# Rotary embedding of the query tiles moved behind the head's softmax bound in a fused attention and feed-forward kernel

## The chip, the cores and the metric

The kernel runs on the 8 cores of one Trainium2 chip. Each core computes one batch element, with no exchange between cores. The metric is the device time of the slowest core, in microseconds (us).

## What is computed

The layer normalises x once and adds attention and a feed-forward block side by side:

```python
xn = _layernorm(x, axis=-1)
x = x + _L0_attn_ref(xn, W_q, W_k, W_v, W_o) + _L0_ffn_ref(xn, w_gate, w_up, w_down, s_gate, s_up, s_down)
# attention: 16 query heads, 4 key/value heads, head size 128, 2048 positions
Qr = _apply_rope(Q, positions)      # r0 = x0*cos - x1*sin ; r1 = x0*sin + x1*cos
Kr = _apply_rope(K_rep, positions)
scores = jnp.einsum('bhqd,bhkd->bhqk', Qr, Kr) / HEAD_DIM ** 0.5
weights = jax.nn.softmax(scores, axis=-1)
out = jnp.einsum('bhqk,bhkd->bhqd', weights, V_rep) @ W_o   # heads joined first
# feed-forward: int8 weights with one scale per output column
gate = silu(_qmatmul(x, w_gate, s_gate)); up = _qmatmul(x, w_up, s_up)
_qmatmul(gate * up, w_down, s_down)
```

## The kernel before, in words

All activations lie transposed, with features on the 128 partitions. The program has three stages. Stage 0 (until about 230 us) loads x, computes the layer norm and transposes it into `xn`. Stage A is K and V projection (until about 376 us) and then attention, head by head. Stage B (from about 1920 us) is the feed-forward block and the output projection over four tiles of 512 positions.

The change lies in the loop over the 16 heads `h` of stage A. One head is built like this:

- **Q projection.** For each tile `t` of 512 positions (NT = 4), 16 matmuls (L421) fill PSUM bank `ps_sc[:, t]`. `norm_max` (L285) then finds the largest squared norm among the tile's query vectors: ScalarE squares the tile (L291), TensorE sums it over partitions with a product by ones (L295, into `ps_sm[0]`, bank 6), and VectorE takes the maximum (L301 for the first tile; L304 and L306 for the others). Before the next such product TensorE claims bank 6, so it waits for that maximum. ScalarE copies the tile to `qps` in SBUF (L427), which frees the bank. `rope_sb` (L273) is the rotary embedding: six VectorE operations (L274, L276, L278, L279, L281, L283) from `qps` into `qr`, by way of `tmp0` and `tmp1`.
- **The bound.** From the maximum over queries and that over the keys (`smal[0, gk]`), VectorE works out a shift for the exponential (L434, L436), TensorE spreads it over the partitions (L440), and VectorE copies it to `bias_h` (L446). The softmax thus needs no maximum of its own.
- **Blocks.** For each block `q` of 512 queries there are four batches `b`. In a batch TensorE computes scores of 512 keys by 512 queries (3 matmuls at L469, one at L464, over all four banks of `ps_sc`), and ScalarE turns them into `expT` (L479). Ahead of each batch's scores TensorE does a quarter of the previous block's work, "pend": 4 matmuls by V (L371, the last at L367, into `ps_av`) and 4 by ones (L384, the last at L380, into `ps_sm`). The previous block may be the last one of the previous head. Behind a block's four batches comes the epilogue of the previous block on VectorE: a reciprocal (L395) and a product (L396).

The order is the order of the code: each engine has a list of closures, filled by the loops and run in order. `ev` appends to VectorE's list and `es` to ScalarE's; with `chain=True` a VectorE operation first waits for the count `sv` of the one before it. `ew(engine, sem, value)` appends a wait, left out when that engine has already waited for as much of the same semaphore. `te_claim(bank)` makes TensorE wait for the bank's last reader. Before the first scores of block `q` stands

```python
if b == 0:
    ew("t", sv, qrope[q])
```

which is the wait for the rotary embedding of tile `q`. In the kernel before it adds nothing, because TensorE has already waited for `negc` (L436), and that stands behind all four embeddings in VectorE's list:

```python
te_claim(6)
ew("t", sv, negc)
bmm = mm_group(1, ...)      # L440
...
bias_done = ev(lambda v: v.tensor_copy(bias_h[:], ps_sm[0][:, 0:1]))
```

The exponentials of a head wait for `bias_done` once, and each waits for its scores.

Of the kernel before, what the change touches and what calls it, by code (L numbers as in the profile page):

```python
# [19 lines left out]
NT = 4  # L20
IC = 64
SBW = 32
TS = 512
# [14 lines left out]
def build_program():  # L38
# [23 lines left out]
    def em(eng, fn):  # L62
        streams[eng].append(fn)

    def ew(eng, sem, val):
        if val > 0 and waited[eng].get(id(sem.h), 0) < val:
            waited[eng][id(sem.h)] = val
            em(eng, lambda e, h=sem.h, v=val: e.wait_ge(h, v))

    stack = contextlib.ExitStack()  # L70
    with stack:
# [3 lines left out]
        ss = mksem("s_s")  # L75
# [33 lines left out]
        ps_sc = stack.enter_context(nc.psum_tensor("ps_sc", [128, 4, 512], F32))  # L109
# [14 lines left out]
        def te_claim(bank):  # L124
            c = psum_free[bank]
            if c is not None:
                ew("t", c[0], c[1])
                psum_free[bank] = None
# [33 lines left out]
        with contextlib.ExitStack() as sa:  # L162
# [93 lines left out]
            qr = sba("qr", [128, S], BF16)  # L256
            qps = sba("qps", [128, 4, 512], BF16)
# [15 lines left out]
            def rope_sb(src, dst_e, dst_o, t0):  # L273
                ev(lambda v, p=src, a=t0: v.tensor_mul(  # L274
                    tmp0[:], p[0:64, :], cos_sb[0:64, a:a + TS]))
                ev(lambda v, p=src, a=t0: v.tensor_mul(  # L276
                    tmp1[:], p[64:128, :], sin_sb[64:128, a:a + TS]))
                ev(lambda v, d=dst_e: v.tensor_sub(d, tmp0[:], tmp1[:]))  # L278
                ev(lambda v, p=src, a=t0: v.tensor_mul(  # L279
                    tmp0[:], p[0:64, :], sin_sb[0:64, a:a + TS]))  # L280
                ev(lambda v, p=src, a=t0: v.tensor_mul(  # L281
                    tmp1[:], p[64:128, :], cos_sb[64:128, a:a + TS]))
                return ev(lambda v, d=dst_o: v.tensor_add(d, tmp0[:], tmp1[:]))  # L283

            def norm_max(src_ap, acc_slot, first, wait_t):  # L285
                par = norm_max.par
                norm_max.par ^= 1
                ew("s", st_, wait_t)
                if norm_max.free[par]:
                    ew("s", st_, norm_max.free[par])  # L290
                sq_done = es(lambda s, p=par, a=src_ap: s.activation(  # L291
                    sqt[p][:], a, AF.Square), chain=False)
                te_claim(6)
                ew("t", ss, sq_done)
                nm = mm_group(1, lambda t_, i, p=par: t_.matmul(  # L295
                    ps_sm[0][0:1, :], ones_bf[:, 0:1], sqt[p][:],
                    start=True, stop=True))
                norm_max.free[par] = nm
                ew("v", st_, nm)
                if first:  # L300
                    rmx = ev(lambda v, sl=acc_slot: v.reduce_max(  # L301
                        smal[0:1, sl:sl + 1], ps_sm[0][0:1, :], axis=AX.X))
                else:
                    ev(lambda v: v.reduce_max(  # L304
                        smal[0:1, 26:27], ps_sm[0][0:1, :], axis=AX.X))
                    rmx = ev(lambda v, sl=acc_slot: v.tensor_max(  # L306
                        smal[0:1, sl:sl + 1], smal[0:1, sl:sl + 1],
                        smal[0:1, 26:27]))
                psum_free[6] = (sv, rmx)
                return sq_done  # L310
# [9 lines left out]
            for t in range(NT):  # L320
                ew("t", stq[t], qdone[t])
                for gk in range(G):
# [7 lines left out]
                    sqd = norm_max(PS(bank), gk, t == 0, kp)  # L330
# [77 lines left out]
            for h in range(H):  # L408
                gk = h // 4
                if h + 1 < H:  # L410
                    if h >= 1:
                        ew("g", st_, qproj_done[h - 1])
                    wq_val[h + 1] = dma(
                        "g", "wq%d" % ((h + 1) % 2), lambda g, i=h + 1,
                        p=(h + 1) % 2: g.dma_start(wq_sb[p][:], wqd[i]))
                ew("t", L["wq%d" % (h % 2)], wq_val[h])
                qrope = [0] * NT
                for t in range(NT):
                    te_claim(t)
                    qp = mm_group(DC, lambda t_, d, tt=t, hh=h:  # L420
                                  t_.matmul(ps_sc[:, tt, :],  # L421
                                            wq_sb[hh % 2][:, d, :],
                                            xn[:, d, tt * TS:tt * TS + TS],
                                            start=(d == 0), stop=(d == DC - 1)))
                    qproj_done[h] = qp
                    sqd = norm_max(ps_sc[:, t, :], 16, t == 0, qp)
                    evv = es(lambda s, tt=t: s.copy(  # L427
                        qps[:, tt, :], ps_sc[:, tt, :]), chain=False)
                    psum_free[t] = (ss, evv)
                    ew("v", ss, evv)  # L430
                    qrope[t] = rope_sb(qps[:, t, :],
                                       qr[0:64, t * TS:t * TS + TS],
                                       qr[64:128, t * TS:t * TS + TS], t * TS)
                ev(lambda v, gg=gk: v.tensor_add(  # L434
                    smal[0:1, 24:25], smal[0:1, 16:17], smal[0:1, gg:gg + 1]))
                negc = ev(lambda v: v.tensor_scalar_mul(  # L436
                    smal[0:1, 25:26], smal[0:1, 24:25], NEG_CBOUND))
                te_claim(6)
                ew("t", sv, negc)
                bmm = mm_group(1, lambda t_, i: t_.matmul(  # L440
                    ps_sm[0][:, 0:1], ones1f[:], smal[0:1, 25:26],
                    start=True, stop=True))
                if exp_last:
                    ew("v", ss, exp_last)
                ew("v", st_, bmm)
                bias_done = ev(lambda v: v.tensor_copy(  # L446
                    bias_h[:], ps_sm[0][:, 0:1]))
                psum_free[6] = (sv, bias_done)
                for q in range(NT):
                    qp = q % 2  # L450
                    exp_b = [0] * 4
                    for b in range(4):
                        if pend is not None:
                            emit_avsums_batch(pend, b)
                        if b == 0:
                            ew("t", sv, qrope[q])
                        for j in range(4):
                            te_claim(j)
                        for j in range(4):
                            kc = 4 * b + j  # L460
                            last = j == 3
                            em("t", lambda t_, jj=j, k=kc, gg=gk, a=q * TS,
                               la=last:
                               (t_.matmul(ps_sc[:, jj, :],  # L464
                                          kr[:, gg, k * 128:k * 128 + 128],
                                          qr[:, a:a + TS], start=True,
                                          stop=True, skip_group_check=True)
                                .then_inc(st_.h, 1)) if la else
                               t_.matmul(ps_sc[:, jj, :],  # L469
                                         kr[:, gg, k * 128:k * 128 + 128],  # L470
                                         qr[:, a:a + TS], start=True,
                                         stop=True, skip_group_check=True))
                        sc_done = st_.inc(1)
                        if q == 0 and b == 0:
                            ew("s", sv, bias_done)
                        if b == 0 and expT_free[qp]:
                            ew("s", st_, expT_free[qp])
                        ew("s", st_, sc_done)
                        exp_b[b] = es(lambda s, p=qp, b0=4 * b: s.activation(  # L479
                            expT[p][:, b0:b0 + 4, :], ps_sc[:, :, :], AF.Exp,  # L480
                            bias=bias_h[:], scale=isq_sb[:]), chain=False)
                        for j in range(4):
                            psum_free[j] = (ss, exp_b[b])
                    exp_last = exp_b[3]
                    exp_last_of[(gk, q, qp)] = exp_last
                    if pend is not None:
                        emit_attn_epilogue(pend, pend_head[0], pend_head[1])
                    pend = (gk, q, qp)
                    pend_head = [h, q]
# [273 lines left out]
```

How the kernel before makes its waits and increments, by code:

```python
    def ew(eng, sem, val):  # L65
        if val > 0 and waited[eng].get(id(sem.h), 0) < val:
            waited[eng][id(sem.h)] = val
            em(eng, lambda e, h=sem.h, v=val: e.wait_ge(h, v))
# [16 lines left out]
        def dma(eng, lane, build):  # L85
            em(eng, lambda e, b=build, h=L[lane].h: b(e).then_inc(h, 16))
            return L[lane].inc(16)
# [1 line left out]
        def ev(build, chain=True):  # L89
            prev = sv.n
            if chain:
                em("v", lambda v, b=build, p=prev: (
                    v.wait_ge(sv.h, p) if p else None,
                    b(v).then_inc(sv.h, 1)))
            else:
                em("v", lambda v, b=build: b(v).then_inc(sv.h, 1))
            return sv.inc(1)
# [1 line left out]
        def es(build, chain=True):  # L99
            prev = ss.n
            if chain:
                em("s", lambda s, b=build, p=prev: (
                    s.wait_ge(ss.h, p) if p else None,
                    b(s).then_inc(ss.h, 1)))
            else:
                em("s", lambda s, b=build: b(s).then_inc(ss.h, 1))
            return ss.inc(1)
# [22 lines left out]
        def mm_group(n, build_i):  # L130
            for i in range(n):
                if i < n - 1:
                    em("t", lambda t_, ii=i: build_i(t_, ii))
                else:
                    em("t", lambda t_, ii=i: build_i(t_, ii).then_inc(st_.h, 1))
            return st_.inc(1)
```

## Time and profile before

| | us |
|---|---|
| median of 3 runs shown | 5054.74 |
| lowest and highest of them | 4822.34, 5358.37 |
| profiled execution, own time | 4829.78 |
| its span on core 4 (the slowest) | 4827.7 |
| spans of the 8 cores | 4794.5 to 4827.7 |
| mean granted TensorE clock of the cores | 0.960 to 0.961 |

The profile shows one execution on core 4. A row of the timeline gives start, duration, engine, source line, operation, what is written and read, the count of merged instructions, and in brackets the idle time ahead of it with what ended it. TensorE's clock is given as the share of full speed that was granted. The duration of one matmul includes its way through the array, so merged matmuls are read by their starts. The durations of the operations of a head are the same to some hundredths of a us in all heads.

### The profile page before, as it was taken

Reading aid. Unit: us, or ns where it says so; the run is one execution under the profiler, and the core shown is the slowest. Engines: PE = TensorE matmul, PEld = TensorE weight load, DVE = VectorE, ACT = ScalarE, POOL = GpSimd, SP = SyncE. Lnnn points to the kernel's source line nnn. Section 1 sums busy time; section 2 is a strip of 40 time slices with the busy share of each in tenths; the row PEclk is TensorE's granted clock in tenths of the full one; section 3 lists DMA queues with packets and bytes.
Section 4 is the critical chain, followed back from the end, with each engine's and each line's share of the span. In section 5 each row is a group of like instructions: output and inputs, shape, how many; then the busy total and the mean of one; then the engine's idle time right before and its main releaser. Section 6 shows DMA issues by size and latency. Waiting matters only on the chain.

```text
span 4827.7 us, 43404 instructions; the slowest of 8 cores (4794.5 to 4827.7 us)
## 1 busy us (share of the span) xinstructions
PE 4055.3 (84%) x17672; PEld 1771.7 (37%) x18032; DVE 1007.5 (21%) x1324; ACT 854.8 (18%) x723; POOL 224.7 (5%) x432
## 2 busy tenths in 40 slices
PE   0186677766776776999999999999999999999999
PEld 0032222222222222444444444444444444444444
DVE  2263433343343333011000111000111000111000
ACT  3203344334433443010000001000001000010000
POOL 0000000000000000000000000000000000000000
PEclk9998898989898898999999999999999999999999
DMA  9800000000000000633355544355634355543354
GB/s 149 191 1 8 14 10 11 10 14 10 11 10 14 11 6 28 234 155 143 147 183 179 205 157 157 131 183 179 216 146 157 137 181 174 205 155 144 130 182 145
DMA packets 139331, 546.07 MB, mean 113 GB/s; under 512 B 43856, under 2 KB 68448, under 8 KB 95616
## 3 DMA queue, kind: packets, MB, share of 16 engines
q0 software_dynamic: 60720, 465.67, 27.7%
q1 hardware_dynamic: 78416, 77.61, 6.4%
q8 instruction: 146, 2.39, 0.2%
q14 instruction: 49, 0.40, 0.0%
HBM read 346.10 MB, written 33.55 MB: 79 GB/s over the span
## 4 chain that ended last, share of the span: by engine, by line
PE 72%; ACT 12%; DVE 9%; DMA 4%; issue 3%; DVEq 0%; another core or an unknown queue 0%; ACTq 0%; POOL 0%; SPq 0%; POOLq 0%
PE ps_sc L591 18%; PE ps_av L637 18%; PE ps_sc L608 18%; ACT expT L479 11%; PE ps_sm L647 5%; PE ps_sc L469 5%; DMA x_t<-x_nat 2%; PE ps_sm L384 2%; PE ps_av L371 2%; PE ps_sc L464 1%; PE ps_sc L421 1%; DVE tmp L281 1%; DVE tmp L276 1%; DVE qr L283 1%; DVE qr L278 1%
## 5 line engine op out<-in xcount | busy, mean ns | idle before, releaser
L591 PE MATMUL ps_sc<-xn_t,wg_sb 128*128 128x512 bf16 x4016 | 922.7, 380 | 31.2 <-DMA xn_t<-xn_scr 26.9
L608 PE MATMUL ps_sc<-xn_t,wu_sb 128*128 128x512 bf16 x4013 | 919.7, 379 | 4.3
L637 PE MATMUL ps_av<-fuse,wd_sb 128*128 128x512 bf16 x4015 | 890.2, 379 | 8.7 <-DVE fuse L617 4.3
L479 ACT ACTIVATE expT<-ps_sc,bias_h,isq_sb 128x2048 bf16<-128x2048 f32 x256 | 526.6, 2057 | 679.7 <-PE ps_sc L464 672.4
L599 ACT ACTIVATE gate_sb<-ps_sc,sg_sb 128x512 bf16<-128x512 f32 x256 | 175.9, 687 | 2417.2 <-PE ps_sc L591 2361.3
L591 PEld LDWEIGHTS ps_sc<-xn_t,wg_sb 128*128 128x128 bf16 x4096 | 401.3, 98 | 512.3 <-issue 30.8
L637 PEld LDWEIGHTS ps_av<-fuse,wd_sb 128*128 128x128 bf16 x4096 | 400.5, 98 | 488.5 <-issue 6.1
L608 PEld LDWEIGHTS ps_sc<-xn_t,wu_sb 128*128 128x128 bf16 x4096 | 400.8, 98 | 483.3
L617 DVE SCALAR_TENSOR_TENSOR fuse<-ps_sc,su_sb,gate_sb 128x512 bf16<-128x512 f32 x256 | 192.1, 751 | 1599.5 <-PE ps_sc L608 1531.8
L395 DVE RECIPROCAL rb_sb<-ps_sm 128x512 f32<-128x512 f32 x64 | 214.9, 3357 | 811.8 <-PE ps_sm L380 811.8
L371 PE MATMUL ps_av<-expT,vtm 128*128 128x512 bf16 x945 | 273.6, 410 | 114.3 <-ACT expT L479 112.7
L469 PE MATMUL ps_sc<-qr,kr 128*128 128x512 bf16 x748 | 233.1, 423 | 116.2 <-ACT expT L479 115.2
L384 PE MATMUL ps_sm<-expT,ones_bf 128*128 128x512 bf16 x934 | 292.3, 438 | 2.0 <-issue 1.3
L421 PE MATMUL ps_sc<-xn,wq_sb 128*128 128x512 bf16 x1004 | 235.4, 385 | 35.9 <-ACT expT L479 34.7
L661 DVE SCALAR_TENSOR_TENSOR out_sb<-ps_av,sd_sb,xT_sb 128x512 f32<-128x512 f32 x64 | 48.0, 750 | 1014.7 <-PE ps_sm L647 949.7
L326 PE MATMUL ps_sc<-xn,wk_sb 128*128 128x512 bf16 x251 | 59.5, 389 | 227.0 <-DMA wv_sb<-wv 226.7
L647 PE MATMUL ps_sm<-attn_t,wo_sb 128*128 128x512 bf16 x1002 | 229.6, 379 | 0.9
L371 PEld LDWEIGHTS ps_av<-expT,vtm 128*128 128x128 bf16 x960 | 94.7, 103 | 251.8 <-issue 167.2
L469 PEld LDWEIGHTS ps_sc<-qr,kr 128*128 128x128 bf16 x768 | 70.4, 108 | 276.6 <-issue 252.0
L540 POOL DMA_DIRECT2D wg_sb<-wg x128 | 67.7, 529 | 1963.5 <-PE ps_sc L608 1562.5
L421 PEld LDWEIGHTS ps_sc<-xn,wq_sb 128*128 128x128 bf16 x1024 | 96.4, 99 | 163.6 <-issue 60.6
L384 PEld LDWEIGHTS ps_sm<-expT,ones_bf 128*128 128x128 bf16 x960 | 103.7, 108 | 140.4 <-issue 48.2
(71 smaller groups left out, 1326.6 us busy)
## 6 DMA issues: line engine op xcount, KB each, us to landing
wg_sb<-wg POOLq DMA_DIRECT2D x128, 1024.0 KB, 4.5
wu_sb<-wu POOLq DMA_DIRECT2D x128, 1024.0 KB, 6.5
wd_sb<-wd POOLq DMA_DIRECT2D x64, 2048.0 KB, 7.4
wo_sb<-wo POOLq DMA_DIRECT2D x64, 512.0 KB, 6.9
x_t<-x_nat POOLq DMA_DIRECT2D x16, 1024.0 KB, 13.9
xT_sb<-xT SPq DMA_DIRECT2D x64, 256.0 KB, 6.3
outT<-out_sb SPq DMA_DIRECT2D x64, 256.0 KB, 6.1
wq_sb<-wq POOLq DMA_DIRECT2D x16, 512.0 KB, 5.0
```

The lines of the kernel that those rows point to most:

```text
L371: t_.matmul(ps_av[p2][:], vtm[:, k, gg * 128:gg * 128 + 128], expT[p2][:, k, :], start=(k == 0), stop=(k == DC - 1), skip_group_check=True))
L384: t_.matmul(ps_sm[p2][:], ones_bf[:], expT[p2][:, k, :], start=(k == 0), stop=(k == DC - 1), skip_group_check=True))
L395: ev(lambda v, p2=pq: v.reciprocal(rb_sb[:], ps_sm[p2][:]))
L421: t_.matmul(ps_sc[:, tt, :], wq_sb[hh % 2][:, d, :], xn[:, d, tt * TS:tt * TS + TS], start=(d == 0), stop=(d == DC - 1)))
L469: t_.matmul(ps_sc[:, jj, :], kr[:, gg, k * 128:k * 128 + 128], qr[:, a:a + TS], start=True, stop=True, skip_group_check=True))
L479: exp_b[b] = es(lambda s, p=qp, b0=4 * b: s.activation(expT[p][:, b0:b0 + 4, :], ps_sc[:, :, :], AF.Exp, bias=bias_h[:], scale=isq_sb[:]), ...
L591: t_.matmul(PS(b), wg_sb[p][:, d, j:j + 128], xn_t[tp][:, d, :], start=(d == 0), stop=(d == DC - 1)))
L599: silu_v = es(lambda s, b=bank, p=ic % 2, i=ic: s.activation(gate_sb[p][:], PS(b), AF.Silu, scale=sg_sb[:, i:i + 1]), chain=False)
L608: t_.matmul(PS(b), wu_sb[p][:, d, j:j + 128], xn_t[tp][:, d, :], start=(d == 0), stop=(d == DC - 1)))
L617: lambda v, b=bank2, p=ic % 2, i=ic: v.scalar_tensor_tensor(fuse[:, i, :], PS(b), su_sb[:, i:i + 1], gate_sb[p][:], ALU.mult, ALU.mult), c ...
L637: t_.matmul(PS(b), wd_sb[p][:, i, :], fuse[:, i, :], start=(i == 0), stop=(i == IC - 1)))
L647: t_.matmul(PS(b), wo_sb[p][:, f, :], attn_t[:, f, :], start=(f == 0), stop=(f == DC - 1)))
```

## The change

The rotary embedding of the four query tiles leaves the Q projection loop. It now stands, for all four tiles in a row, behind the copy to `bias_h`, ahead of the blocks. Nothing is computed differently. ScalarE's list is the same; VectorE's has the same instructions in another order; TensorE's has the same instructions and, before the first scores of each block, a wait for `qrope[q]` that is no longer covered by an earlier one.

```diff
                     qproj_done[h] = qp
-                    sqd = norm_max(ps_sc[:, t, :], 16, t == 0, qp)
+                    norm_max(ps_sc[:, t, :], 16, t == 0, qp)
                     evv = es(lambda s, tt=t: s.copy(
                         qps[:, tt, :], ps_sc[:, tt, :]), chain=False)
                     psum_free[t] = (ss, evv)
-                    ew("v", ss, evv)
-                    qrope[t] = rope_sb(qps[:, t, :],
-                                       qr[0:64, t * TS:t * TS + TS],
-                                       qr[64:128, t * TS:t * TS + TS], t * TS)
+                qps_done = ss.n
...
                 psum_free[6] = (sv, bias_done)
+                ew("v", ss, qps_done)
+                for t in range(NT):
+                    qrope[t] = rope_sb(qps[:, t, :],
+                                       qr[0:64, t * TS:t * TS + TS],
+                                       qr[64:128, t * TS:t * TS + TS], t * TS)
                 for q in range(NT):
```

On VectorE, from the maximum over the last query tile of a head to the end of the head's preparation, this stood in a row before:

```order
L304 TENSOR_REDUCE smal<-ps_sm 1x1
L306 TENSOR_TENSOR smal<-smal 1x1
L274 TENSOR_TENSOR tmp<-qps,cos_sb 64x512
L276 TENSOR_TENSOR tmp<-qps,sin_sb 64x512
L278 TENSOR_TENSOR qr<-tmp 64x512
L279 TENSOR_TENSOR tmp<-qps,sin_sb 64x512
L281 TENSOR_TENSOR tmp<-qps,cos_sb 64x512
L283 TENSOR_TENSOR qr<-tmp 64x512
L434 TENSOR_TENSOR smal<-smal 1x1
L436 TENSOR_SCALAR smal<-smal 1x1
L446 COPY bias_h<-ps_sm 128x1
```

And this stands there after the change (L431, L433 and L443 are the former L434, L436 and L446):

```order
L304 TENSOR_REDUCE smal<-ps_sm 1x1
L306 TENSOR_TENSOR smal<-smal 1x1
L431 TENSOR_TENSOR smal<-smal 1x1
L433 TENSOR_SCALAR smal<-smal 1x1
L443 COPY bias_h<-ps_sm 128x1
L274 TENSOR_TENSOR tmp<-qps,cos_sb 64x512
L276 TENSOR_TENSOR tmp<-qps,sin_sb 64x512
L278 TENSOR_TENSOR qr<-tmp 64x512
L279 TENSOR_TENSOR tmp<-qps,sin_sb 64x512
L281 TENSOR_TENSOR tmp<-qps,cos_sb 64x512
L283 TENSOR_TENSOR qr<-tmp 64x512
```

The bound's operations follow the last maximum directly, and the six operations of tile 0 stand behind the copy; those of tiles 1 to 3, eighteen more, follow them. The three embeddings that stood between the earlier maxima of the head are gone from there too.

On TensorE, from the product that spreads the bound to the second batch of a head (any but the first), this stood before; `s_s` counts ScalarE's operations and `s_v` VectorE's:

```order
L440 MATMUL ps_sm<-smal,ones1f 128x1 [waits s_v]
L371 MATMUL ps_av<-expT,vtm 128x512 x4
L384 MATMUL ps_sm<-expT,ones_bf 128x512 x4
L469 MATMUL ps_sc<-qr,kr 128x512 [waits s_s]
L469 MATMUL ps_sc<-qr,kr 128x512 x2
L464 MATMUL ps_sc<-qr,kr 128x512
```

And this stands there now (L437, L471 and L466 are the former L440, L469 and L464):

```order
L437 MATMUL ps_sm<-smal,ones1f 128x1 [waits s_v]
L371 MATMUL ps_av<-expT,vtm 128x512 x4
L384 MATMUL ps_sm<-expT,ones_bf 128x512 x4
L471 MATMUL ps_sc<-qr,kr 128x512 [waits s_v,s_s]
L471 MATMUL ps_sc<-qr,kr 128x512 x2
L466 MATMUL ps_sc<-qr,kr 128x512
```

No matmul has moved; the first scores have a wait for VectorE of their own.

## Rows read from the trace of the kernel before

**Rows 1.** The page of the slowest core: granted clock in 40 slices, in tenths.

```profile
PEclk9998898989898898999999999999999999999999
```

**Rows 2.** By stretch: length, PE, PEld, DVE, ACT, POOL busy; clock; DMA share, GB/s.

```profile
380.00:1920.00 1540.00, 1064.65 (x4092) 416.05 (x4176) 579.75 (x672) 596.29 (x385) 7.40 (x14) 0.89 0.05 11
876.40:886.00 9.60, 0.48 (x2) 0.50 (x2) 7.62 (x14) 0.00 (x0) 0.00 (x0) 0.66 0.33 55
886.00:889.60 3.60, 3.60 (x10) 1.34 (x10) 0.16 (x1) 0.00 (x0) 0.00 (x0) 0.50 0.00 0
```

**Rows 3.** Timeline, preparation of the sixth head on core 4, all engines.

```profile
857.15 3.61 PE L421 MATMUL ps_sc<-xn,wq_sb 128*128 128x512 bf16 x16 [2.30 <-ACT expT L479]
...
861.60 0.38 PE L295 MATMUL ps_sm<-sqt,ones_bf 128*1 128x512 bf16 x1 [0.84 <-ACT sqt L291]
...
862.15 0.68 DVE L301 TENSOR_REDUCE smal<-ps_sm 1x1 f32<-1x512 f32 x1 [4.50 <-PE ps_sm L295]
...
875.92 0.38 PE L295 MATMUL ps_sm<-sqt,ones_bf 128*1 128x512 bf16 x1 [0.84 <-ACT sqt L291]
...
879.21 0.68 DVE L304 TENSOR_REDUCE smal<-ps_sm 1x1 f32<-1x512 f32 x1
879.99 0.15 DVE L306 TENSOR_TENSOR smal<-smal 1x1 f32<-1x1 f32 x1
880.24 0.68 DVE L274 TENSOR_TENSOR tmp<-qps,cos_sb 64x512 f32<-64x512 bf16 x1
...
884.98 0.15 DVE L434 TENSOR_TENSOR smal<-smal 1x1 f32<-1x1 f32 x1
885.23 0.14 DVE L436 TENSOR_SCALAR smal<-smal 1x1 f32<-1x1 f32 x1
885.52 0.55 PE L440 MATMUL ps_sm<-smal,ones1f 1*128 1x1 f32 x2 [9.22 <-DVE smal L436]
886.01 1.89 PE L371 MATMUL ps_av<-expT,vtm 128*128 128x512 bf16 x4
886.25 0.16 DVE L446 COPY bias_h<-ps_sm 128x1 f32<-128x1 f32 x1 [0.87 <-PE ps_sm L440]
...
889.40 0.96 PE L469 MATMUL ps_sc<-qr,kr 128*128 128x512 bf16 x3
...
890.67 2.06 ACT L479 ACTIVATE expT<-ps_sc,bias_h,isq_sb 128x2048 bf16<-128x2048 f32 x1 [14.42 <-PE ps_sc L464]
...
892.87 0.81 PE L469 MATMUL ps_sc<-qr,kr 128*128 128x512 bf16 x3 [0.57 <-ACT expT L479]
```

**Rows 4.** Timeline of TensorE: block starts in the sixth head, then the seventh's Q projection.

```profile
902.84 1.41 PE L371 MATMUL ps_av<-expT,vtm 128*128 128x512 bf16 x4 [2.30 <-ACT expT L479]
...
919.55 1.05 PE L371 MATMUL ps_av<-expT,vtm 128*128 128x512 bf16 x4 [2.30 <-ACT expT L479]
...
952.65 3.61 PE L421 MATMUL ps_sc<-xn,wq_sb 128*128 128x512 bf16 x16 [2.30 <-ACT expT L479]
```

**Rows 5.** Busy time by stretch: after a block start, and after that Q projection's start.

```profile
903.40:906.60 3.20, 3.20 (x9) 1.03 (x7) 0.00 (x0) 0.00 (x0) 0.00 (x0) 0.50 0.15 46
952.70:956.20 3.50, 3.50 (x16) 1.41 (x16) 0.45 (x1) 0.00 (x0) 0.00 (x0) 1.00 0.11 37
```

**Rows 6.** Timeline of TensorE: first Q projection tile of the second head.

```profile
472.54 5.30 PE L421 MATMUL ps_sc<-xn,wq_sb 128*128 128x512 bf16 x16 [2.30 <-ACT expT L479]
```

**Rows 7.** Timeline of the first head, which has no earlier block to work off.

```profile
394.78 0.38 PE L295 MATMUL ps_sm<-sqt,ones_bf 128*1 128x512 bf16 x1 [0.84 <-ACT sqt L291]
...
404.88 1.03 PE L469 MATMUL ps_sc<-qr,kr 128*128 128x512 bf16 x2
...
410.34 1.44 PE L469 MATMUL ps_sc<-qr,kr 128*128 128x512 bf16 x3 [3.58 <-ACT expT L479]
...
412.30 2.06 ACT L479 ACTIVATE expT<-ps_sc,bias_h,isq_sb 128x2048 bf16<-128x2048 f32 x1 [2.10 <-PE ps_sc L464]
```

**Rows 8.** Timeline of VectorE: the first epilogue in the sixth head.

```profile
899.19 3.36 DVE L395 RECIPROCAL rb_sb<-ps_sm 128x512 f32<-128x512 f32 x1 [12.79 <-PE ps_sm L380]
```

## The prediction, made before the changed kernel was run

> **What bounds the kernel now.** I read the page first, then the busy time by stretch, then the timeline of one head. On the page the reader sees a granted clock that is lower in places through the first 16 slices, that is in attention, and full behind it [rows 1]. The change touches attention alone. There TensorE is busy for 1064.65 of 1540 us, VectorE for 579.75 and ScalarE for 596.29 [rows 2]: no engine is full, so the time is made by waits, and the question is which wait ends last at the place of the change.
>
> The timeline of the sixth head shows it [rows 3]. From the head's first Q matmul at 857.15 the fourth norm product (L295) is reached at 875.92. VectorE takes 0.55 us to react to such a product (861.60 to 862.15), so it could begin the last maximum at 876.47. It begins it at 879.21, because the embeddings of the earlier tiles stand ahead of it, and then does the fourth tile's embedding, six operations in 884.98 - 880.24 = 4.74 us, before it turns to the bound. TensorE waits 9.22 us for L436, and VectorE is busy for 7.62 us of that stretch [rows 2, 3]. So here the chain is VectorE's. Then come L440 at 885.52, eight matmuls of the previous block from 886.01, the scores at 889.40 and the first exponential at 890.67, which had been waited for 14.42 us. From the exponential on, the block runs at the pace of scores and exponential in turn. The next head begins at 952.65 [rows 4], a period of 95.50 us.
>
> **The change part by part.** Nothing is added or removed as work: 24 VectorE operations per head move behind the copy to the bias, and the wait for tile 0's embedding becomes real.
>
> *The Q projection.* TensorE's pace there is set by matmuls and by ScalarE's squares: the wait ahead of L295 is 0.84 us and ends with the square, not with VectorE [rows 3]. Maxima that come earlier gain nothing here: price 0. The copies to qps are on ScalarE and don't move.
>
> *The bound.* The last maximum begins at 876.47. Its own step is 0.78 us (879.21 to 879.99), the next 0.25 (879.99 to 880.24), from L434 to L436 0.25, from L436 to the product 0.29 (885.23 to 885.52). L440 then begins at 876.47 + 0.78 + 0.25 + 0.25 + 0.29 = 878.04, 7.48 us earlier than before.
>
> *What is late next.* The embedding of tile 0. The bias copy begins 0.73 us after L440 (885.52 to 886.25), at 878.77; a small operation's step is 0.25, so tile 0 begins at 879.02 and its six operations end their steps at 883.76. TensorE sees the end about as a small step later does, 883.8. The eight matmuls in between start at 878.04 + 0.49 = 878.53 and take at most the 3.39 us that they took at the 1.2 GHz level (886.01 to 889.40, granted 0.50 [rows 2, 3]), until 881.92; they are hidden at either level. The scores thus begin at 883.8 instead of 889.40: 5.6 us earlier. The 7.48 us of the bound shrink by what was moved in front of the scores.
>
> *Scores to first exponential.* In this head it was 1.27 us (889.40 to 890.67), where the clock rose on the way. All at the low level it was 1.96 (410.34 to 412.30) [rows 7]. TensorE has now two short waits instead of a long one (876.3 to 878.0, and up to 883.8), and these rows don't say at which level the scores run. The gain to the exponential is therefore 5.6 at best and 5.6 - 0.69 = 4.9 at worst. I take 5.2, a little nearer to the low level, since a pause stands right in front of the scores.
>
> *The other tiles.* Tiles 1 to 3 need 3 x 4.74 = 14.2 us more of VectorE, until about 898.0. Tile 1 is ready at 888.5, and block 1 began at 902.84 [rows 4], some 5 us earlier now: still late by 9. The first epilogue began at 899.19 [rows 8] and would have begun near 894; now it waits for VectorE until 898 and, with the 3.36 of its reciprocal and some 0.8 for the product, ends at about 902.2. Its banks are claimed at the start of block 2 (919.55 before [rows 4], some 914 now). Cover 12 us: price 0. Nothing else is queued behind it that TensorE needs.
>
> *The clock further on.* This is the term that I can't read off the operations. Each of the four block ends of a head leaves TensorE idle for the same 2.30 us [rows 4], and after the block starts the matmuls run at the low level, 0.50 from 903.40 to 906.60 (and likewise in the two blocks after), while after the fourth such pause, ahead of the next head's Q projection, the clock is 1.00 [rows 5]. Of the 15 first Q tiles behind such a pause on core 4, two ran at the low level, in the second and third head: the row shows the second's, 5.30 us against 3.61 [rows 3, 6]. The same pause is thus followed by either level, and this one is spared by where it falls. A shift by 5 us against the Q projection moves all of them, and nothing in the rows protects the fourth. Its price is 5.30 - 3.61 = 1.69 us per head, bounds 0 (as in most heads now) and 1.69; on the other side a block start that is now slow could be spared, also worth about 1.7 at most. I take the full 1.69 as a cost and no gain, because three of four such pauses are slow today and the one spared is the one that has nothing more to win.
>
> The Trainium skill, page "TensorE: Matmul & The Clock Gate", section "HAM oscillation — how this bites in real kernels", says that matmul groups that start after long waits each start at the low clock, and advises keeping TensorE from waiting so that this cost goes away. Splitting the 9.22 us wait would by that rule give back the slow restart. The trace agrees that the matmuls behind that wait run at 0.50 [rows 2], but it shows the same after pauses of 2.30 us [rows 4, 5], and pauses of this size remain. I keep the rule as a rival.
>
> *The sum.* Per head 5.2 - 1.69 = 3.5 us, for 15 heads 52.5. The first head has no eight matmuls between bound and scores. There L440 would begin at 394.78 + 0.55 + 0.78 + 0.25 + 0.25 + 0.29 = 396.90, the embedding of tile 0 ends 0.73 + 0.25 + 4.74 later, and the scores begin at about 402.7 instead of 404.88 [rows 7]: 2.2 us. Stage B begins when the last head ends and runs as before. Total 54.7, and 4829.78 - 54.7 = 4775. The sum is made against the profiled execution (own time 4829.78, span 4827.7), near the lowest of the three runs shown (4822.34); their median, 5054.74, lies 4.7% above it, and no row of the profile holds those 225 us, so I don't build on it.
>
> **The rivals.**
>
> *The clock is kind (4730).* By the rule above, and by the spared Q tile of today, the fourth pause stays free and one block start or the restart is freed too. Then a head gains 5.6 to 5.6 + 1.7 = 7.3; 15 x 6.5 + 2.2 = 100, and 4730. For it: the level after equal pauses does differ. Against it: three of four are slow now, and it needs two favourable turns in most heads.
>
> *Only the Q tile is spared (4750).* 15 x 5.2 + 2.2 = 80, and 4829.8 - 80 = 4750. For it: 13 of 15 first Q tiles were spared before.
>
> *The embedding only changes its place in the chain (4830).* If VectorE's operations behind the bias took longer than before, or a wait hid in front of tile 0 (ScalarE's last copy, done at about 876.3), the scores would come as late as now. Against it: the copy stands right behind the square that the product at 875.92 waited for, 3 us ahead of 879.02, and the six operations depend on nothing else.
>
> *Slower: the low clock stays (4856).* In the first head the second batch's scores still run low, three in 1.44 us [rows 7] against 0.81 at 892.87 [rows 3]. A low batch with its eight other matmuls has 12 at 3.39 / 8 = 0.42 us, 5.1, with the hand-over 5.2, against the 3.47 from the first scores to the second now (889.40 to 892.87). The place is the first block of each head: if the short pauses ahead of the scores kept the level low through four batches more than today, that costs 4 x 1.73 = 6.9 against 5.2 gained, and 1.7 x 15 = 26 slower with the first head's gain lost too, 4856. It decides from 5.2 / 1.73 = 3 extra slow batches per head. Against it: behind a much longer wait the level rises again within the first scores (three in 0.96 us), once TensorE has worked without a pause, and with eight more matmuls in every batch it is not starved as in the first head.
>
> **How the numbers follow.** Forecast (4775; 4769 to 4780 by the 5.6 and the 4.9) 0.62; Q tile spared 0.15; kind clock 0.14; no gain 0.05; slower 0.04. About 2% is what a measurement of this kernel can tell from no change, 97 us, so faster by over 2% needs under 4733: most of the kind-clock case and a little beside it, 0.13. Slower by over 2% would need over 4926, beyond the price of every rival here: 0.02. Within 2%: 0.85. The range leaves out the slower end and the outer half of the kind case: 4725 to 4815.
>
> **What would show it.** Right: the L436 successor's product near 20.9 us after the head's first matmul (28.4 now) where that tile ran at full speed, the scores 26.6 after it (32.25 now), TensorE's new wait ended by the embedding's last operation (L283), the period near 92 us instead of 95.5, and first Q tiles of 5.3 us in most heads. Wrong: a period near 95 (embedding as late as before), near 89 or less (kind clock), batches 5 us apart in the first block (low clock stays), or a wait of TensorE at block 1 or 2 for VectorE (the epilogue's cover was thinner than worked out).

## The result, and the profile after

The changed kernel is faster: the ratio to the kernel before is 0.9852, 95% interval 0.9833 to 0.987. On the 4829.78 us of the profiled execution before that is 71 us (63 to 81); the forecast was 54.7. The median of its ten runs is 4782.7 us and that of the kernel before, over ten runs, 5069.51. Both medians contain executions in which the cores of one die ran at a lower clock; the ratio leaves those out.

The profiled execution after has an own time of 4741.86 us and a span of 4740.3 on core 6, 87.4 less than the span before. Not all of that belongs to the change. From the timelines: the first Q matmul is at 358.8 instead of 376.0 (17.2 us, from the stages ahead of attention, where the change does nothing and the eight cores lie up to 30 us apart in one execution), from there to the last product of attention it is 1471.3 instead of 1539.3 us (68.0), and behind that 2.2. Over the eight cores attention takes 1466.8 us on average against 1539.6: 72.8 us, near the 71 of the ratio.

The waits of TensorE in the stretch of attention, of the kernel before on core 4; the columns are the waiting engine and group, what it waited for, us in total, times, longest:

```profile
PE ps_sm L440 <- DVE smal L436: 148.1, 16, 9.6
PE ps_sc L469 <- ACT expT L479: 114.1, 190, 3.6
PE ps_av L371 <- ACT expT L479: 110.4, 48, 2.3
PE ps_sm L295 <- ACT sqt L291: 54.0, 64, 1.1
PE ps_sc L421 <- ACT expT L479: 34.7, 15, 2.5
```

The same of the changed kernel, core 6:

```profile
PE ps_av L371 <- ACT expT L481: 112.7, 49, 2.3
PE ps_sc L471 <- ACT expT L481: 105.5, 177, 3.6
PE ps_sc L471 <- DVE qr L283: 53.4, 16, 5.3
PE ps_sm L295 <- ACT sqt L291: 52.3, 62, 1.1
PE ps_sc L421 <- ACT expT L481: 34.5, 15, 2.3
PE ps_sm L437 <- DVE smal L433: 28.6, 16, 2.1
```

The wait for the bound fell from 148.1 to 28.6 us, and a new one, of the scores for the embedding, took 53.4. The waits for the exponentials are near what they were (259.2 and 252.7 us in sum), and so are those for the squares. The difference, 148.1 - 28.6 - 53.4 = 66.1 us, is not the time gained by itself, since the matmuls around the waits run at either clock level.

The timeline of one head after the change, core 6 (all engines, some rows), answers to [rows 3]:

```profile
820.95 5.30 PE L421 MATMUL ps_sc<-xn,wq_sb 128*128 128x512 bf16 x16 [2.30 <-ACT expT L481]
...
841.41 0.38 PE L295 MATMUL ps_sm<-sqt,ones_bf 128*1 128x512 bf16 x1 [0.84 <-ACT sqt L291]
841.96 0.68 DVE L304 TENSOR_REDUCE smal<-ps_sm 1x1 f32<-1x512 f32 x1 [3.84 <-PE ps_sm L295]
842.74 0.15 DVE L306 TENSOR_TENSOR smal<-smal 1x1 f32<-1x1 f32 x1
...
843.53 0.35 PE L437 MATMUL ps_sm<-smal,ones1f 1*128 1x1 f32 x2 [1.75 <-DVE smal L433]
843.81 1.04 PE L371 MATMUL ps_av<-expT,vtm 128*128 128x512 bf16 x4
844.06 0.16 DVE L443 COPY bias_h<-ps_sm 128x1 f32<-128x1 f32 x1 [0.67 <-PE ps_sm L437]
844.32 0.68 DVE L274 TENSOR_TENSOR tmp<-qps,cos_sb 64x512 f32<-64x512 bf16 x1
...
849.21 1.44 PE L471 MATMUL ps_sc<-qr,kr 128*128 128x512 bf16 x3 [3.49 <-DVE qr L283]
...
851.17 2.06 ACT L481 ACTIVATE expT<-ps_sc,bias_h,isq_sb 128x2048 bf16<-128x2048 f32 x1 [9.43 <-PE ps_sc L466]
```

VectorE is idle ahead of the last maximum now (3.84 us) and reacts 0.55 us after the fourth norm product begins. From that product the bound's product follows after 2.12 us and the scores after 7.80; worked out were 2.12 and 7.88. The three short waits are to be seen: 1.75 us for the bound, 3.49 us for the embedding (the eight matmuls in between ran at full speed), and 2.30 us ahead of this head's first Q tile, which then took 5.30 us as in [rows 6].

The busy time by stretch gives the clock level in that head: in the first Q tile, behind the product for the bound, and at the start of block 1 (length; PE, PEld, DVE, ACT, POOL busy; granted clock; DMA):

```profile
821.00:824.00 3.00, 3.00 (x10) 1.12 (x11) 0.45 (x1) 0.00 (x0) 0.00 (x0) 0.63 0.13 44
844.00:846.00 2.00, 1.71 (x8) 0.59 (x6) 1.63 (x4) 0.00 (x0) 0.00 (x0) 1.00 0.72 143
864.00:866.00 2.00, 2.00 (x6) 0.70 (x5) 2.00 (x1) 0.00 (x0) 0.00 (x0) 0.50 0.00 0
```

The first Q tile and the start of block 1 run mostly or wholly at 1.2 GHz, the eight matmuls behind the bound at 2.4.

**All heads.** I took the same marks from the timelines of all eight cores for the second to the sixteenth head: 120 first Q tiles, 112 whole periods. Means in us, counted from the head's first Q matmul; a first Q tile counts as low if it took near 5.3 instead of 3.6:

| | first Q tile low | bound's product | first scores | first exponential | first to last exponential | period |
|---|---|---|---|---|---|---|
| before | 24 of 120 | 28.78 | 32.65 | 33.94 | 59.62 | 95.77 |
| after | 74 of 120 | 22.01 | 27.72 | 29.68 | 59.20 | 91.09 |

A head is 4.68 us shorter, and 15 x 4.68 = 70.2; the remainder of the 72.8 is the first head. Of the 4.68 us, 4.26 lie ahead of the first exponential and 0.42 in the blocks.

The 0.42 is the sum of two larger changes with opposite signs. Each of the 112 heads has three steps from a block's last exponential to the next block's first, 336 in all. Such a step takes 5.0 us where the matmuls after the pause run at full speed and mostly 6.3 to 6.7 where they don't. Before, 16 of the 336 were near 5.0, after the change 91: 1.07 us less per head. Against it, the step from a head's first exponential to its second, 3.32 us in every head before, is 3.97 on average, because the low level behind the new wait lasts, in half of the heads, through the matmuls that follow the first scores too (57 of 112 steps are longer, up to 4.7 us).

### The profile page after: what moved, and what is told of

It is laid out like the page before. It is cut to its first block, busy times and chain, and to the rows that moved or that the text cites. A ratio compares the mean times of both kernels' runs of the same rounds, so it can differ in the third digit from the quotient of the medians.

```text
span 4740.3 us, 43748 instructions; the slowest of 8 cores (4720.1 to 4740.3 us)
## 1 busy us (share of the span) xinstructions
PE 4084.9 (86%) x18032; PEld 1769.0 (37%) x18032; DVE 1007.5 (21%) x1324; ACT 854.9 (18%) x723; POOL 225.0 (5%) x432
## 4 chain that ended last, share of the span: by engine, by line
PE 78%; ACT 12%; DVE 4%; DMA 3%; issue 2%; DVEq 0%; ACTq 0%; POOL 0%; SPq 0%; POOLq 0%
PE ps_sc L593 19%; PE ps_av L639 19%; PE ps_sc L610 19%; ACT expT L481 11%; PE ps_sc L421 5%; PE ps_sc L471 5%; PE ps_sm L649 5%; PE ps_av L371 2%; PE ps_sm L384 2%; DMA x_t<-x_nat 2%; PE ps_sc L466 1%; DMA wv_sb<-wv 1%; ACT sqt L291 1%; PE ps_av L341 1%; PE ps_sm L295 1%
## 5 line engine op out<-in xcount | busy, mean ns | idle before, releaser
L471 PE MATMUL ps_sc<-qr,kr 128*128 128x512 bf16 x768 | 237.6, 423 | 159.1 <-ACT expT L481 105.5
L421 PE MATMUL ps_sc<-xn,wq_sb 128*128 128x512 bf16 x1024 | 253.8, 405 | 34.5 <-ACT expT L481 34.5
L471 PEld LDWEIGHTS ps_sc<-qr,kr 128*128 128x128 bf16 x768 | 67.5, 105 | 319.0 <-issue 290.8
```

The lines of the kernel that those rows point to most:

```text
L421: t_.matmul(ps_sc[:, tt, :], wq_sb[hh % 2][:, d, :], xn[:, d, tt * TS:tt * TS + TS], start=(d == 0), stop=(d == DC - 1)))
L471: t_.matmul(ps_sc[:, jj, :], kr[:, gg, k * 128:k * 128 + 128], qr[:, a:a + TS], start=True, stop=True, skip_group_check=True))
```

## Experiments

Ratios are to the kernel before, measured beside it. "Period" and the other marks are the means over heads and cores, taken as above from each profiled execution.

**1. Tile 0's embedding back in the loop.**

```diff
                     psum_free[t] = (ss, evv)
+                    if t < 1:
+                        ew("v", ss, evv)
+                        qrope[t] = rope_sb(...)
...
-                for t in range(NT):
+                for t in range(1, NT):
                     qrope[t] = rope_sb(...)
```

> The changed kernel with tile 0's embedding put back into the Q projection loop, right behind its copy; tiles 1 to 3 stay behind the bias copy. Theory A (what is left after the change is the wait of the first scores for tile 0's embedding): the bound's product stays 20.9 us after the head's first matmul, the scores come right behind the eight matmuls, at 20.9 + 0.49 + 1.7 to 3.4 = 23.1 to 24.8 instead of 26.6, so 1.8 to 3.5 us less per head than the changed kernel, 28 to 55 us in all, ratio to before 0.974 to 0.980. Rival B (the embedding only stood beside TensorE's own work and the clock's cost): scores still near 26.6, ratio 0.985 as the changed kernel.

Measured: ratio 0.9716 (0.9701 to 0.9731), first scores at 24.40, first exponential 25.89, period 87.00. The head prepares like this:

```profile
824.62 0.35 PE L442 MATMUL ps_sm<-smal,ones1f 1*128 1x1 f32 x2 [1.75 <-DVE smal L438]
824.90 1.04 PE L371 MATMUL ps_av<-expT,vtm 128*128 128x512 bf16 x4
825.77 1.52 PE L384 MATMUL ps_sm<-expT,ones_bf 128*128 128x512 bf16 x4
827.09 1.49 PE L476 MATMUL ps_sc<-qr,kr 128*128 128x512 bf16 x3
829.10 2.06 ACT L486 ACTIVATE expT<-ps_sc,bias_h,isq_sb 128x2048 bf16<-128x2048 f32 x1 [6.27 <-PE ps_sc L471]
```

The scores follow the eight matmuls without a wait, and the bound is as early as before the edit. The new wait was the limit. The gain over the changed kernel, 15 x 4.09 = 61 us, is a little more than the 28 to 55 expected: 3.32 came from the scores, the other 0.8 from matmuls that ran at the upper level more often behind them (1.48 from scores to exponential instead of 1.96, and 3.32 again from the first exponential to the second).

**2. Tile 0's embedding last of the four.**

```diff
-                for t in range(NT):
+                for t in (1, 2, 3, 0):
                     qrope[t] = rope_sb(...)
```

> The changed kernel with the four embeddings behind the bias copy in the order 1, 2, 3, 0. Theory A: the scores of block 0 wait for three more embeddings, 3 x 4.74 = 14.2 us: scores 40.8 us after the head's first matmul, period about 91.1 + 14.2 = 105.3 against 95.8 before, some 150 us slower than before, ratio 1.03. Rival B (the wait for tile 0 is covered by other work): less than 14.2 per head, ratio below 1.02.

Measured: ratio 1.0343 (1.0321 to 1.0365), period 106.10, and in heads with a full-speed first Q tile the scores at 40.90. TensorE's new wait, one head:

```profile
491.41 0.35 PE L437 MATMUL ps_sm<-smal,ones1f 1*128 1x1 f32 x2 [1.75 <-DVE smal L433]
...
511.45 1.44 PE L471 MATMUL ps_sc<-qr,kr 128*128 128x512 bf16 x3 [17.35 <-DVE qr L283]
513.41 2.06 ACT L481 ACTIVATE expT<-ps_sc,bias_h,isq_sb 128x2048 bf16<-128x2048 f32 x1 [23.80 <-PE ps_sc L466]
```

Three more embeddings in front of the scores cost 14.24 us there (40.90 against 26.66), as 3 x 4.74 = 14.2 says. The period rose by 0.8 more than that, in the blocks (60.4 instead of 59.20). Nothing hides VectorE's work at this place.

**3. Three embeddings in the loop, the fourth behind the bias.** The edit is that of the first experiment with 3 for 1.

> The changed kernel with the embeddings of tiles 0, 1 and 2 in the Q projection loop and only tile 3's behind the bias copy. Theory A: the last maximum waits for the backlog as in the kernel before (it begins 22.06 us after the head's first matmul instead of 19.3), the bound's product comes at 23.6, the scores at 25.8 to 27.5; so the backlog costs 2.7 us per head against the version with tile 0 alone in the loop, ratio 0.980 to 0.988 against 0.9716. Rival (only the order of tile 0 counts): 0.972.

Measured: ratio 0.9852 (0.9825 to 0.9879), period 91.38. The bound's product comes at 23.67 in heads with a full-speed first tile, and TensorE waits 4.50 us for it instead of 1.75:

```profile
843.27 0.38 PE L295 MATMUL ps_sm<-sqt,ones_bf 128*1 128x512 bf16 x1 [0.84 <-ACT sqt L291]
848.14 0.55 PE L442 MATMUL ps_sm<-smal,ones1f 1*128 1x1 f32 x2 [4.50 <-DVE smal L438]
```

So both parts of the old chain count: the fourth embedding ahead of the bound, and the backlog of the earlier ones ahead of the last maximum. Its period is 4.4 us above that with tile 0 alone in the loop, 2.7 of it from the bound; most of the rest is the eight matmuls behind the bound, which now follow a longer pause (3.84 us on average from the bound's product to the scores, against 2.30). The ratio is that of the change as made.

**4. Filler in the pause ahead of the Q projection.** Here a bank of the row sums, free at that time, takes eight products that nobody reads; the result is computed as before.

```diff
                     pend = (gk, q, qp)
                     pend_head = [h, q]
+                    if q == NT - 1 and h + 1 < H:
+                        te_claim(6 + qp)
+                        for i in range(8):
+                            em("t", lambda t_, p2=qp: t_.matmul(
+                                ps_sm[p2][:], ones_bf[:], xn[:, 0, 0:TS], ...))
```

> The changed kernel with 8 filler matmuls (ones by a part of xn, into a bank that is free) ahead of each head's Q projection, in the 2.30 us for which TensorE waits there. Theory A (a first Q tile at 1.2 GHz is a consequence of the idle pause ahead of it): no first Q tile of 5.30 us, period lower by the about 0.5 x 1.69 = 0.85 us that they cost on average now, some 13 us in all, ratio about 0.9825. Rival C (the level there is set by where it falls in the head and not by the pause): half of the tiles still 5.30, ratio 0.985 or higher.

Measured: ratio 0.9844 (0.9814 to 0.9874), which can't be told from 0.9852. But no first Q tile of 120 was low:

```profile
820.75 1.89 PE L495 MATMUL ps_sm<-xn,ones_bf 128*128 128x512 bf16 x8
821.01 2.06 ACT L481 ACTIVATE expT<-ps_sc,bias_h,isq_sb 128x2048 bf16<-128x2048 f32 x1 [1.27 <-PE ps_sc L466]
823.21 3.61 PE L421 MATMUL ps_sc<-xn,wq_sb 128*128 128x512 bf16 x16 [0.57 <-ACT expT L481]
```

The low tile is a consequence of the pause. Yet of the 1.29 us that the first exponential gained (28.39), 0.63 was lost again in the blocks (59.83 from first to last exponential), and the period fell by 0.66, to 90.43, where 0.85 was expected. Nearly all of the loss lies at the block ends, which this edit doesn't touch: 54 of their 336 steps were near 5.0 us instead of 91.

**5. Filler at the end of every block.** The condition of the fourth experiment is `if True`.

> As the one before, with the 8 filler matmuls at the end of every block. Theory A: the matmuls at block starts run at 2.4 GHz too, 1.7 instead of 3.4 us for eight, so three times 1.7 per head and the 0.85 of the Q tile, about 6 us per head, 90 us in all, ratio about 0.967. Rival C: no change against the changed kernel, 0.985, or slower where filler stands in the way of the scores' successor.

Measured: ratio 0.9689 (0.9669 to 0.971). The marks are those of cores 0 to 3, since cores 4 and 5 took 17 to 20 us longer for attention than the other six in this execution: period 86.37, blocks 55.49 (86.56 and 55.60 over all eight). Every step over a block's end took 5.05 us. A block start behind filler, eight matmuls in 1.73 us (921.43 to 923.16):

```profile
918.97 1.89 PE L495 MATMUL ps_sm<-xn,ones_bf 128*128 128x512 bf16 x8
921.43 1.02 PE L371 MATMUL ps_av<-expT,vtm 128*128 128x512 bf16 x4 [0.57 <-ACT expT L481]
922.29 1.03 PE L384 MATMUL ps_sm<-expT,ones_bf 128*128 128x512 bf16 x4
923.16 0.81 PE L471 MATMUL ps_sc<-qr,kr 128*128 128x512 bf16 x3
```

More work for TensorE made a head 4.7 us shorter; about 6 were expected. Low stretches behind the wait for the embedding remain (1.95 us from scores to first exponential).

**6. The same filler in the kernel before.** The edit of the fifth experiment, made in the kernel before.

> The kernel before with the 8 filler matmuls at the end of every block, to be set against the changed kernel with the same filler (ratio 0.969, period 86.6, blocks 55.6 from first to last exponential). Theory A (the operations give 5.0 us per head to the first exponential; the rest of the difference between the two kernels is the clock's share): first Q tiles at full speed, first exponential 33.5 us after the head's first matmul as before, blocks near 55.6, period about 33.5 + 55.6 + 2.2 = 91.3, ratio about 0.986, and 4.7 to 5 us per head above the changed kernel with filler. Rival E (the change's gain came from the clock): the two filled kernels are within 1 us per head.

Measured: ratio 0.9808 (0.9727 to 0.9888), no low first tile, first exponential at 33.97, blocks 55.05, period 91.23, as expected; every step over a block's end took 5.05 us here too. The interval of the ratio is wide, and the argument rests on the marks. Set against the fifth they show the change with the pauses at block ends filled on both sides: 91.23 - 86.37 = 4.86 us per head (4.67 over all eight cores). So the gain of the change comes from the order of the operations and not from the clock; the rival falls.

**7 and 8. One or two more VectorE operations ahead of tile 0's embedding.**

```diff
                 ew("v", ss, qps_done)
+                for _ in range(2):      # one in experiment 7
+                    ev(lambda v: v.tensor_mul(
+                        tmp0[:], qps[0:64, 0, :], cos_sb[0:64, 0:TS]))
```

> The changed kernel with one more VectorE operation (a repeated product into tmp0) between the bias copy and tile 0's embedding. Theory A by operations alone: scores 0.79 us later in each head, period 91.1 + 0.8 = 91.9, 12.6 us more in all, ratio 0.988. Theory A with the clock's share as a term of its own: the scores are 0.79 later after a tile at full speed, but the share of first Q tiles at 1.2 GHz changes too, by up to some tenths, each tenth 0.17 us per head, so the period lies between 91.2 and 92.5.

> The changed kernel with two more VectorE operations between the bias copy and tile 0's embedding (with one more the period rose by 1.45 us, from 91.09 to 92.54). By operations alone: scores 1.58 us later, period 92.7. Theory A with the clock as a term of its own: scores 28.2 after the head's first matmul where that tile was at full speed, and a period that isn't 1.58 higher but anywhere from 91.5 to 94.5.

Measured from the profiled executions (own times 4771.61 and 4793.06 against 4741.86; no ratio to the kernel before was taken for these two). The scores moved by 0.79 and by 1.55 us after full-speed tiles (27.45 and 28.21 against 26.66), but the period by 1.45 (92.54) and by 2.92 (94.01). The first period lies just above the range I had named (91.2 to 92.5), the second within its own. Low first tiles were 53 and 64 of 120, fewer than the 74 without delay, while the blocks grew from 59.20 to 60.14 and 60.71. A microsecond of VectorE at this place cost nearly two, and the surplus lies at the block ends: of the 336 steps there, 91 were near 5.0 us without delay, 39 with one operation more and none with two, which costs 0.92 and 1.42 us per head.

**9. Scores ahead of the previous block's matmuls.**

```diff
                     for b in range(4):
-                        if pend is not None:
-                            emit_avsums_batch(pend, b)
                         if b == 0:
                             ew("t", sv, qrope[q])
...
                         sc_done = st_.inc(1)
+                        if pend is not None:
+                            emit_avsums_batch(pend, b)
```

> The changed kernel with each batch's scores ahead of the previous block's eight matmuls on TensorE. Theory A (what is left at a block start is eight matmuls at the low clock between an exponential and the next scores): the step from a block's last exponential to the next block's first falls from 6.7 to the 3.3 us of any other, 3 x 3.4 = 10 us per head, period about 81 instead of 91.1; the first exponential of a head doesn't move, since the scores wait for tile 0's embedding at 26.6 us either way. In all 15 x 15 + 12 = 235 us below before, ratio about 0.951. Rival D (TensorE's own work is then the bound, 12 matmuls a batch): period not under 88, ratio 0.97 or higher.

Measured: ratio 0.955 (0.9523 to 0.9578), period 81.86, blocks 51.06, no first Q tile low. The step over a block's end is 3.32 us, like any other, as expected. In experiment 5, where only the low level was gone, it was 5.05, so 3 x (5.05 - 3.32) = 5.2 of the 9.2 us per head come from the eight matmuls that no longer stand ahead of the scores. The other 4.0 are the clock's: the same eight matmuls now stand where the pause was, and the wait ahead of the next head's Q projection is 0.57 us instead of 2.30:

```profile
784.69 3.61 PE L421 MATMUL ps_sc<-xn,wq_sb 128*128 128x512 bf16 x16 [0.57 <-ACT expT L481]
```

**10. Both: scores first, and tile 0's embedding in the loop.**

> The one before, and tile 0's embedding back in the Q projection loop. Theory A: now nothing stands between the bound and the scores; they begin at 20.9 + 0.5 = 21.4 us after the head's first matmul and the first exponential at 22.5 to 23.4, 5 to 6 us earlier than with the embedding behind the bias, period about 75.5, 85 us less than the one before, ratio about 0.933. Rival B (the embedding's place no longer matters): same as the one before.

Measured: ratio 0.9344 (0.9319 to 0.9368), first exponential at 22.94, period 75.56, own time 4497.15, as expected. It beats both kernels by far. Bound, scores and exponential of one head:

```profile
845.74 0.35 PE L442 MATMUL ps_sm<-smal,ones1f 1*128 1x1 f32 x2 [1.75 <-DVE smal L438]
846.02 0.86 PE L474 MATMUL ps_sc<-qr,kr 128*128 128x512 bf16 x3
846.26 0.16 DVE L448 COPY bias_h<-ps_sm 128x1 f32<-128x1 f32 x1 [0.67 <-PE ps_sm L442]
846.67 0.63 PE L469 MATMUL ps_sc<-qr,kr 128*128 128x512 bf16 x1
847.40 2.06 ACT L486 ACTIVATE expT<-ps_sc,bias_h,isq_sb 128x2048 bf16<-128x2048 f32 x1 [3.46 <-PE ps_sc L469]
```

ScalarE waits 3.46 us where it waited 14.42 before [rows 3].

## Why the prediction was right in its chain and wrong in one term

- **What bounds the head: right.** VectorE's queue held the bound back. The bound's product came 20.90 us after the head's first matmul where the first tile was at full speed, against 28.37 before: 7.47 us, forecast 7.48. (These and the figures of the next two points are medians of such heads; their means lie up to 0.1 us higher.) Experiments 1 to 3 show both parts of that queue.
- **What is late next: right.** The scores wait for tile 0's embedding, at 26.58 in such heads (forecast 26.6). Experiments 1 and 2 move that one wait either way with the price worked out for it.
- **Scores to first exponential: sized a little high.** I took a gain of 5.2 us between 4.9 and 5.6. It was 33.52 - 28.54 = 4.98, since the scores behind the new wait ran at the low level: 1.96 us as the mean of 112 heads. It lies next to my lower bound, 4.9.
- **Q projection, tiles 1 to 3, epilogue at no cost: right.** TensorE doesn't wait for VectorE at any later block; the list of waits has 16 for the embedding, one per head. The epilogue begins when the last embedding ends, 863.26 in the head shown, and nobody waits for it:

```profile
862.47 0.69 DVE L283 TENSOR_TENSOR qr<-tmp 64x512 bf16<-64x512 f32 x1
863.26 3.36 DVE L395 RECIPROCAL rb_sb<-ps_sm 128x512 f32<-128x512 f32 x1
```

- **The clock further on: this is the step that failed.** I charged the first Q tile of every head with the full 1.69 us and put the blocks at nothing. For the tile the direction was right: the share of low first tiles rose from 24 to 74 of 120. But it rose by 0.42, so the term was 0.42 x 1.69 = 0.70 us, not 1.69. And the blocks held two terms that I had left out: the steps over block ends, 1.07 us shorter because more of them were spared (91 of 336 instead of 16), and the first step of a head, 0.65 longer because of the low level behind the new wait. Together the blocks became 0.42 shorter. Per head: 4.98 - 0.70 + 0.42 = 4.70 (measured 4.68), where the forecast had 3.5. Times 15 the miss is 18 us, and 54.7 + 18 = 73 is what attention gained. The reason I gave, that nothing protects the fourth pause, only says that it may be hit, not that it always is. I should have priced a share, with both ends in the range. Even the count at hand was misread: the prediction has two low first tiles on core 4, the trace has three (24 of 120 over all eight cores). The third is the tenth head's:

```profile
1237.74 5.30 PE L421 MATMUL ps_sc<-xn,wq_sb 128*128 128x512 bf16 x16 [2.30 <-ACT expT L479]
```

- **The time and what could be told.** By the ratio the changed kernel stands at 4758 us on the profiled execution's time, inside 4725 to 4815, 17 from the 4775 named. The gain of 1.5% lies within 2%, the case that had the largest chance. But I had called 2% about what a measurement tells from no change, and that was wrong here: the interval of the ratio is 0.2% to either side and the change is clear of it. I should have said "faster by one to two per cent" and meant it as a change. Making the sum against the profiled execution, and not against the median of 5054.74, was right.
- **The rivals.** The measured 4758 lies between the spared Q tile (4750), which assumes no low tile, and the forecast (4775), which assumes that all are low; 62% were. The kind clock (4730) came true in part, with 91 of 336 block starts spared. The low clock that stays through the first block came true for a part of one batch in half of the heads and not for the four that it needed. The embedding did not keep its old price.

The rule of the Trainium skill that I had set against my sum (page "TensorE: Matmul & The Clock Gate", section "HAM oscillation — how this bites in real kernels": groups that start after long waits start at the low clock, so keep TensorE from waiting) was of the right kind. The filler experiments bear it out, with pauses of 2.30 us: with those at block ends filled, no first Q tile took 5.3 us and blocks took 55.49 instead of 59.20 us. What the change did not do is fill pauses: it made one long one into two short ones, and the one right ahead of the scores was followed by the low level (1.96 us to the first exponential).

What stays open: what decides which of a head's equal pauses is followed by the low level when nothing is filled. The counts change with each edit (first Q tiles 24, 74, 53 and 64 of 120, full-speed block starts 16, 91, 39 and 0 of 336, for before, after and the two delays). That the delays cost nearly double follows from the second row of counts; why the counts are what they are isn't shown.

## What to carry to other kernels

When work is moved behind a small but urgent result on an in-order engine, ask which piece of it is the next thing waited for, and leave exactly that piece in front: tile 0's embedding in the loop and three behind was worth nearly twice the change as made (8.8 against 4.7 us per head). Where the clock follows the engine's pauses, price a low stretch by the share of places where it occurs, counted over all cores, and not by its presence at one. And before trimming a chain that feeds a burst of matmuls, look at the order within the burst: putting the scores ahead of the old block's products removed 9 us per head, 4 of them because those products then filled the pause.

## What was not expected of the hardware

Eight extra matmuls per block, 1.9 us of pure added TensorE work each time, made both kernels faster, by 4.7 and 4.5 us per head (91.09 to 86.37, and 95.77 to 91.23), because the matmuls behind them ran at 2.4 instead of 1.2 GHz. Filled at one pause only, the same trick gave half back at the others (1.29 us gained at the first exponential, 0.63 lost in the blocks). And a delay of 0.79 us on VectorE cost 1.45 us per head, one of 1.55 us cost 2.92, the surplus being block starts that had run at full speed and no longer did.
